# Normalising one batch's 4x4 matrices inside the other batch's attention

## The reference

```python
def step(carry, _):
    u, v = carry
    u = -jax.nn.logsumexp(Z + v[..., None, :], axis=-1)
    v = -jax.nn.logsumexp(Z + u[..., :, None], axis=-2)
    return ((u, v), None)
(u, v), _ = jax.lax.scan(step, (u0, v0), None, length=num_iters)
H_res = jnp.exp(Z + u[..., :, None] + v[..., None, :])
...
H_res = (1.0 - g) * I + g * H_res
x_pre = jnp.einsum('btnc,btn->btc', x_streams, H_pre)
y = x_pre @ W_branch
x_mixed = jnp.einsum('btij,btjc->btic', H_res, x_streams)
y_distributed = jnp.einsum('btc,btn->btnc', y, H_post)
return (x_mixed + y_distributed).reshape(B, T, nC)
```

## Time and profile before

| what | value |
|---|---|
| median of 3 runs | 2467.94 us (2463.57 to 2469.21) |
| the profiled execution, its own time | 2463.85 us |
| its span | 2461.6 us |
| PE busy | 2233.0 us (91%) |
| DVE busy | 1554.9 us (63%) |
| ACT busy | 1046.4 us (43%) |
| POOL busy | 1012.0 us (41%) |
| mean bandwidth | 67 GB/s, DMA engines 18.8% busy |
| chain that ended last | PE 32%, DVE 2%, issue 1%, ACT 1% of the span |

### The profile page before, as it was taken

How to read it: one execution, slowest core, us unless ns; L and a number is a source line. 1 busy time by engine, 2 the same in 40 slices (tenths; PEclk the granted TensorE clock), 3 DMA queues, 4 the chain that set the end, 5 groups by cost and what they waited for, 6 DMA issues and landing times. The chain is left out here.

```text
span 2461.6 us, 35450 instructions
## 1 busy us (share of the span) xinstructions
PE 2233.0 (91%) x11154; PEld 1814.2 (74%) x11154; DVE 1554.9 (63%) x3685; ACT 1046.4 (43%) x2182; POOL 1012.0 (41%) x1038
## 2 busy tenths in 40 slices
PE   5767449899999999999999796999999999999998
PEld 4633137688888888888887684788888888888886
DVE  4289875466666666666766455566565756566665
ACT  4322213354545444454545232444454545454543
POOL 2644351264545455363634100435262525343341
PEclk9878779899999999999999998999999999999999
DMA  9500035501010101101010434201101010101010
GB/s 341 189 9 1 0 140 209 207 26 66 9 65 9 65 26 48 56 17 56 26 48 1 166 131 185 86 27 43 47 21 51 26 56 13 60 9 60 18 38 31
DMA packets 74003, 164.83 MB, mean 67 GB/s; under 512 B 4704, under 2 KB 38880, under 8 KB 67296
## 3 DMA queue, kind: packets, MB, share of 16 engines
q1 hardware_dynamic: 73504, 162.69, 18.8%
q10 hardware_dynamic: 432, 1.32, 0.1%
HBM read 113.14 MB, written 72.61 MB: 75 GB/s over the span
## 5 line engine op out<-in xcount | busy, mean ns | idle before, releaser
L1521 DVE TENSOR_TENSOR pT<-psum,pT 128x512 fp32r<-128x512 f32 x576 | 387.0, 689 | 282.4 <-ACT pT L1562 281.6
L1474 POOL TENSOR_TENSOR probs_even<-probs_even,rinv 128x1024 f32<-128x1024 f32 (+2 forms) x192 | 241.0, 1255 | 677.5 <-DVE rinv L1512 677.5
L1562 ACT ACTIVATE pT<-psum 128x512 fp32r<-128x512 f32 x576 | 329.2, 596 | 299.1 <-PE psum L1615 299.0
L1507 DVE CUSTOM_DVE_ANT_0 psum<-psum,causal 128x256 f32<-128x256 f32 (+7 forms) x512 | 386.0, 767 | 38.1 <-PE psum L95 33.3
L1474 POOL TENSOR_TENSOR probs_odd<-probs_odd,rinv 128x896 f32<-128x896 f32 (+2 forms) x192 | 198.6, 1042 | 303.0 <-DVE rinv L1512 302.9
L1556 ACT ACTIVATE probs_even<-psum,nmax 128x1024 f32<-128x1024 f32 (+3 forms) x256 | 204.5, 799 | 250.1 <-DVE nmax L1507 246.2
L93 PE MATMUL psum<-keys,q 128*128 128x512 f32 (+3 forms) x768 | 265.6, 346 | 3.7 <-DVE q L1495 2.8
L95 PE MATMUL psum<-keys,q 128*128 128x512 f32 (+3 forms) x768 | 262.0, 341 | 0.0
L94 PE MATMUL psum<-keys,q 128*128 128x512 f32 (+3 forms) x768 | 261.9, 341 | 0.0
L93 PE MATMUL psum<-pT,vals 128*128 128x512 f32 x576 | 256.3, 445 | 3.9
L1556 ACT ACTIVATE probs_odd<-psum,nmax 128x896 f32<-128x896 f32 (+3 forms) x256 | 176.7, 691 | 148.1 <-DVE nmax L1507 145.9
(11 more groups left out here) (272 smaller groups left out, 4410.5 us busy)
## 6 DMA issues: line engine op xcount, KB each, us to landing
k_parts<-kv_out SPq DMA_DIRECT2D x32, 512.0 KB, 4.9
wq<-wq_copy SPq DMA_DIRECT2D x16, 1024.0 KB, 4.8
wo<-wo_copy SPq DMA_DIRECT2D x16, 1024.0 KB, 4.8
v_parts<-kv_out SPq DMA_DIRECT2D x32, 512.0 KB, 3.9
keys<-k_parts SPq DMA_DIRECT2D x32, 512.0 KB, 4.8
vals<-v_parts SPq DMA_DIRECT2D x64, 256.0 KB, 3.1
acc<-in_x SPq DMA_DIRECT2D x4, 1024.0 KB, 12.3
xn_later<-xn SPq DMA_DIRECT2D x1, 2048.0 KB, 14.5
```

Source lines behind the costliest of these rows:

```text
L1474: pool.tensor_tensor(p, p, rinv[:, u, h:h + 1].to_broadcast([P, (TB - u) * P]), ALU.mult).then_inc(p_ok, 1)
L1507: dve.tensor_tensor_reduce(out=row, in0=row, in1=causal[:, S - n:S], scale=-1.0, scalar=-2 * MASKED, op0=ALU.add, op1=ALU.min, accum_out=n ...
L1521: dve.tensor_tensor(pT[:, n % PT_SLOTS, 1, :], bank[T_BANK + n % 2], f32(pT[:, n % PT_SLOTS, 0, :]), ALU.subtract).then_inc(t_lo, 1)
L1562: act.activation(pT[:, n % PT_SLOTS, 0, :], bank[T_BANK + n % 2], ACT.Copy).then_inc(t_hi, 1)
```

## The change

Only batch 0's eight tiles are normalised in `layer0_mix`; a part of the loop is now 4 tiles (128x64 elements). `PER_UNIT` becomes 27 and the additions come at 14 to 17. The additions that fall after half round 98 (tile 11's and the last unit's) are done between the steps of the mixing. Of the mixing of batch 0, DVE keeps six tiles, and POOL gets tiles 6 and 7 (`BY_POOL`), 20 instructions of 128x512. The matrices of batch 1 are centred here but their 98 half rounds run in batch 0's attention: 20 in each of the iterations 0, 1, 3 and 4 and 18 in iteration 2 (`LATER_HALVES`). POOL does the product after a normalisation of heads 0 to 2, from block 1 on (block 2 on in iteration 2), and DVE the sum and the reciprocal (`factor`) behind its own reciprocal of the next such head. After 40 half rounds DVE folds the factors into `z1` (`recentre`), with ACT's Ln and Exp, and in iteration 5 it finishes the matrices (`finish`). The mixing of batch 1's eight tiles, on POOL as before, is gathered in iterations 5 (three tiles), 6 (three) and 7 (two); a pair now comes after each head of 0 to 2 from block 1 on, with two pauses of no work after each tile. DVE's and ACT's iterations of batch 0 are written out.

```diff
+LATER_CHUNKS, LATER_HALVES = (20, 29), (20, 20, 18, 20, 20)
...
+        Z, K = sb("sk_z", [P, NT, NS, NS]), sb("sk_k", [P, TB, NS, NS])
...
-        PER_UNIT = 23
+        PER_UNIT = 27
+        BY_POOL = 2
...
+            pool.wait_ge(mix_ok, 1)
+            for t in range(TB - BY_POOL, TB):
+                x = x1[:, t, :].rearrange("p (i c) -> p i c", i=NS)
+                pool.wait_ge(x1_ok, t + 1)
+                for j in range(NS + 1):
+                    n = 2 * ((NS + 1) * (t - (TB - BY_POOL)) + j)
+                    stream = xn[:, t, j * D:(j + 1) * D] if j < NS else y[:, t, :]
+                    weight = T[:, t, :, j] if j < NS else rw[:, t, 1, :]
+                    if j == NS:
+                        pool.wait_ge(y_ok, t // 4 + 1)
+                    if n:
+                        pool.wait_ge(pooled, n)
+                    pool.tensor_tensor(product[:], stream.unsqueeze(1).to_broadcast([P, NS, D]),
+                                       weight.unsqueeze(2).to_broadcast([P, NS, D]), ALU.mult).then_inc(pooled, 1)
+                    pool.wait_ge(pooled, n + 1)
+                    pool.tensor_tensor(x, x, product[:], ALU.add).then_inc(pooled, 1)
...
+            after(dve.tensor_tensor(Z[:, 0:TB], Z[:, 0:TB], wide_cols(v[:, 0:TB]), ALU.subtract))
+            after(dve.tensor_tensor(m.z1[:], Z[:, TB:NT], wide_cols(v[:, TB:NT]), ALU.subtract))
...
-                behind = PER_UNIT * (unit + 1) + 16 if unit + 1 < UNITS else 2 * sum(CHUNKS) - UQ
-                between.setdefault(behind + k, []).append((add_heads, t))
+                between.setdefault(PER_UNIT * (unit + 1) + 14 + k, []).append((add_heads, t))
...
+            ours = T[:, 0:TB]
+            after(dve.tensor_tensor(ours, K[:], wide_rows(row[:, 0:TB]), ALU.mult))
+            after(dve.tensor_tensor(ours, ours, wide_cols(col[:, 0:TB]), ALU.mult))
...
-            for k in range(0, TB, 2):
+            mixes, at = 0, 2 * sum(CHUNKS)
+            ready = {t: (x1_ok, t + 1) for t in range(NT)}
+            for k in range(0, TB - BY_POOL, 2):
                 for j in range(NS + 1):
                     for t in (k, k + 1):
...
+                        ready[t] = mixed, mixes
+                        for step, unit_tile in between.pop(at, ()):
+                            step(unit_tile)
+                        at += 1
...
-                        if t == 8:
-                            logs()
...
+                if unit == 1:
+                    logs()
...
+            tiles_of = {5: (0, 1, 2), 6: (3, 4, 5), 7: (6, 7)}
...
+                return iter(range(sum(LATER_HALVES[:it]), sum(LATER_HALVES[:it + 1])))
...
-            def loads(it, g):
...
                 load(wq[:, 1], m.wq_s[g]).then_inc(wq_in, 16)
+                for t in mixed_now[:2]:
+                    later_loads(t + 1)
...
+                for t in mixed_now[2:]:
+                    later_loads(t + 1)
...
+                loads(it, it + 1, tiles_of.get(it, ()) if mixes_later else ())
+            if mixes_later:
+                later_loads(TB - 1)
...
-                    yield
                     pool.wait_ge(mixed, n + 1)
                     pool.tensor_tensor(x, x, product[:], ALU.add).then_inc(mixed, 1)
                     yield
...
-                        if h == REP - 2 and 2 <= u:
-                            next(beside, None)
+                        if mixes_later and u >= first_pause(it):
                             next(beside, None)
...
+            def scaling(it):
+
+                for half in halves_of(it):
+                    if half == 2 * LATER_CHUNKS[0]:
+                        pool.wait_ge(k_ok, 1)
+                    pool.wait_ge(factor_ok, factors(half))
+                    pool.tensor_tensor(T1, m.k1[:], over_rows(m.row1) if half % 2 else over_cols(m.col1), ALU.mult).then_inc(scaled, 1)
+                    yield
+
+            def mixings(it):
+                if it == mixing_from:
+                    pool.wait_ge(share_ok, 1)
+                for t in tiles_of[it]:
+                    yield from mixing(t)
+                    yield
+                    yield
...
+                    body(it, it == ITERS - 1, scaling(it) if it < mixing_from else mixings(it))
...
+            def factor(half):
+
+                dve.wait_ge(scaled, half + 1)
+                by = T1 if half % 2 == 0 else T1.rearrange("p t i j -> p t j i")
+                dve.tensor_reduce(m.sm1[:], by, AX.X, ALU.add).then_inc(summed, 1)
+                dve.wait_ge(summed, half + 1)
+                dve.reciprocal((m.col1 if half % 2 else m.row1)[:], m.sm1[:]).then_inc(factor_ok, 1)
...
+            def recentre():
...
+                dve.tensor_tensor(m.z1[:], m.z1[:], over_rows(m.lrow1), ALU.add).then_inc(z_ok, 1)
...
+                dve.tensor_tensor(m.z1[:], m.z1[:], over_cols(m.lcol1), ALU.add).then_inc(z_ok, 1)
+                dve.memset(m.col1[:], 1.0).then_inc(factor_ok, 1)
...
+            def finish():
...
+                dve.wait_ge(factor_ok, factors(halves))
+                dve.tensor_tensor(T1, m.k1[:], over_rows(m.row1), ALU.mult).then_inc(share, 1)
...
+                dve.tensor_tensor(T1, T1, over_cols(m.col1), ALU.mult).then_inc(share, 1)
...
+                dve.tensor_scalar(mix, mix, m.gate[:, 2:3], None, ALU.mult).then_inc(share, 1)
...
+                dve.tensor_scalar(mix[:, :, 0:NZ:NS + 1], mix[:, :, 0:NZ:NS + 1], m.gate[:, 3:4], None, ALU.add).then_inc(share_ok, 1)
...
+                        if mixes_later and (u, h) == (1, 0):
+                            if it == turning:
+                                recentre()
+                            if it == mixing_from:
+                                finish()
                         if h == REP - 1:
 
                             p = probs[u % 2][:, h, 0:(TB - u) * P]
                             dve.wait_ge(p_inv, it * SC + (REP * u + h + 1))
                             dve.tensor_scalar(p, p, rinv[:, u, h:h + 1], None, ALU.mult).then_inc(p_last, 1)
+                        if mixes_later and (h < REP - 1 or u == TB - 1) and (u, h) > (first_pause(it), 0):
+                            half = next(beside, None)
+                            if half is not None:
+                                factor(half)
...
+            if mixes_later:
+                dve.memset(m.col1[:], 1.0).then_inc(factor_ok, 1)
+                for it in range(ITERS):
+                    body(it, it == ITERS - 1, halves_of(it))
...
+                        if mixes_later and it == turning and (u, h) == (1, REP - 1):
+                            act.wait_ge(z_ok, 2)
+                            act.activation(m.k1[:], m.z1[:], ACT.Exp).then_inc(k_ok, 1)
...
+                for it in range(ITERS):
+                    if it == turning:
+                        act.wait_ge(factor_ok, factors(2 * LATER_CHUNKS[0] - 1) + 1)
+                        act.activation(m.lrow1[:], m.row1[:], ACT.Ln).then_inc(logs_ok, 1)
+                        act.activation(m.lcol1[:], m.col1[:], ACT.Ln).then_inc(logs_ok, 1)
+                    body(it, it == ITERS - 1)
```

87 lines of the change are left out of this document (53 added, 34 removed).

## The result

The changed kernel takes 2486.14 us (median of 4 runs, 2485.34 to 2487.2) where the kernel before takes 2468.57 (4 runs, 2463.57 to 2471.56): ratio 1.0073, 95% interval 1.0056 to 1.0091. It is slower, as forecast, and 9 us under the 2495 of the forecast. Spans of the profiled executions: 2461.6 before, 2483.4 after, 21.8 more.

A forecast was written before the change was run, and what follows sets the result against it. DVE was taken to bound the first stage's mixing, PE the attention. First stage 15 us less (-28 + 13), attention 43 more: +28 on the median 2467.94 gives 2496, stated as 2495 us, range 2468 to 2514.

The forecast's parts named there:

- The half rounds: First stage's loop: smaller parts shorten each of 97 half rounds by 0.29 us, 28 us less (19 to 34).
- Zero in sum: First stage's additions: three earlier calls wait 4 us in all, the last unit's 4.39 us wait goes; no net change.
- The mixing: Batch 0's mixing: DVE's 30 us and POOL's 23.4 exclude each other, so 53.4 us, 13.4 more than before.
- Iterations 0 to 4: Batch 0's attention: half rounds in DVE's list delay PE's inputs; 20 us over iterations 0, 1, 3, 4, plus 5 in iteration 2.
- The last normalisation in block 7: Attention, block 7: three factors and another POOL wait ahead of it delay PE; 1.2 us counted per iteration.
- Iteration 2: Batch 0's attention: `recentre` beside POOL's normalisation costs 1.5 us in block 1, block 7 costs 1.8; 5 us taken.
- The cause named for blocks 2 to 4: Attention: a factor ahead of the last low copy makes PE wait; 0.6 us in block 2, 0.5 in 3 and 4.
- Lockstep: Rival, attention: factors and products wait for each other in every block, 10 us more an iteration, 2520 us; chance 0.1.
- Iterations 5 to 7: Batch 0's attention: POOL's mixing pairs delay the last wo part, 5 us stall each; with later blocks and `finish`, 18 us.

The follow-up runs named there:

- pool_mixes_four: Against the changed kernel, GpSimd mixes four of batch 0's tiles instead of two, DVE four, and the last unit's additions come slightly earlier; 2498.46 us.
- psum_operand: Against the changed kernel, DVE's 120 mixing operations read the operand they add to from PSUM, not SBUF, leaving out a sum over streams; 2466.15 us.
- no_half_rounds: Against the changed kernel, batch 1's 98 half rounds and the refolding are left out of the attention on POOL, DVE and ACT; 2464.90 us.
- pairs_from_block2: Against the changed kernel, POOL's mixing pairs in iterations 5 to 7 begin in block 2, not 1, with one pause per tile; 2482.29 us, ratio 1.0069.

## Why the prediction was right, and where it was off

The large terms came from the mechanisms that were named, and the experiments show them. Some single amounts came out right by errors that cancel, as is said at each.

*The half rounds.* Right in its parts; the term was short by 0.04 us a half round, 97 x 0.33 = 32 in place of 28. The three durations fell by 0.31, the handovers by the rest.

*"Zero in sum" for the additions* was wrong. They waited 2.15, 2.15 and 2.02 us, not 1.3, so 6.3 against the 4.39 that went: 2 us more. And I counted five additions neither as leaving the loop (-3.3) nor as arriving in the mixing (+3.3).

*The mixing.* The phase took about the 53.4 us predicted, but by luck: three errors cancel. Before, it lasted 42.1 us, not 40: I read 40.00 busy in a window that I had cut at 328.3, while the last operations ran to 330.4. The row itself counts 153 instructions, not 160. So the operations take 0.263 and 120 of them 31.6. The additions add 3.3. And the exclusion costs 18.6, not 23.4, because about one DVE operation comes through per POOL instruction. That the two exclude each other was right, and its price a quarter too high; the difference against before was +11.4, not +13.4. By the Trainium skill ("SBUF — State Buffer", section "Who interferes with whom") whoever issues first keeps the shared pair for its instruction. The trace agrees for both POOL operations, at 1.26 us per DVE operation against 0.26, and so does the kernel with one input in PSUM, which that rule leaves out of the conflict. POOL loses too, as the rule allows, but little: its three multiplications of 1.17 and 1.18 us in place of 1.05 began just behind a DVE operation, seven of 20 are as slow in pool_mixes_four, and none in psum_operand. An operation of 0.34 us holds POOL up for 0.12, an instruction of 1.05 to 1.26 holds DVE up for 0.9.

*Iterations 0 to 4.* 25 us predicted, 24.7 measured, and no_half_rounds gives all of it to the half rounds. By blocks of iteration 1, from when PE starts the same matmul in both kernels: 1.5 in block 1 (1.9 predicted), 0.6, 0.5, 0.6 and 0.4 in blocks 2 to 5 (0.6, 0.5, 0.5 and 0.3), 0.6 in block 6 (nothing) and 0.7 in block 7 (1.2). The path in blocks 6 and 7 was another than I had: factors ahead of a maximum and an addition make the addition late, and a query projection waits for it. The last normalisation in block 7, which I had blamed, delayed nothing that stayed. So the right sum of blocks 6 and 7 is luck. Iteration 2 lost 4.6 (5 predicted), of it 0.6 in block 1, where I had put 1.5 for `recentre`. The cause named for blocks 2 to 4, a factor ahead of the last low copy, was right and incomplete: the experiment that took it away met the same loss by way of the third maximum and ACT. Lockstep did not happen.

*Iterations 5 to 7.* 18 us predicted, 18.6 measured (7.7, 6.9, 4.0), or 20.1 if the last is taken to the end of the attention alone (5.5). The wait was 4.4 to 4.7, near the 5 predicted. What I had not counted is the clock behind it, 1.4 to 1.6 each time. In the last iteration two more things came, neither counted. PE has three waits there that no engine ends ("issue" in its timeline), 5.9 us together before and 3.7 now, which gave 2.1 back. And the last projection ran for 1.5 us longer at a lower clock. With `finish` ahead of them, the waits for low copies in block 1 of iteration 5 came to 1.3, some 1.0 more than in the kernel before; 1.2 had been put down for it.

*From the profile to the median.* I added the sum to the median and assumed that the profiled execution would again lie 4 us below it. It lay 0.8 below. Of the 9 us between forecast and result some 6 are terms of the sum (the spans differ by 21.8, not 28) and the rest is this.

## To carry to other kernels

Work put into an engine that is idle a third of the time is free or costly by its place alone: list the gaps of the in-order queue in the trace, put one piece into each, and follow a delay through every engine whose list it enters, since here a late maximum came back as a late copy on another engine. Before work is handed to GpSimd beside DVE, look at where both read: with two SBUF operands on DVE, each GpSimd instruction of 1.2 us took 0.93 us from DVE, and none with one operand in PSUM. When a phase is timed by a window, see that the window holds all of it and nothing else.

## What was not expected of the hardware

A stall of PE can cost more than itself. In iteration 5 of the changed kernel PE waited 4.38 us, until 1083.39; then the granted clock fell:

```profile
1054.60:1083.40 28.80, 23.02 (x125) 18.81 (x123) 21.03 (x42) 15.56 (x29) 23.81 (x19) 1.00 0.10 36
1083.40:1088.40 5.00, 5.00 (x17) 4.04 (x18) 0.00 (x0) 0.00 (x0) 3.58 (x3) 0.66 0.00 0
```

From 1084.0 to 1087.6 a pass of 512 columns took up to 0.63 us in place of 0.39 (mean clock 0.66 in the window, so mostly the lower level of 1.2 GHz). From the start of the projection to PE's next transposition it took 4.44 us (1083.39 to 1087.83), in the kernel before 2.84 (1074.68 to 1077.52): 1.6 us lost again. It is not the same each time: in the eight kernels that have these three waits the stretch took 4.2 to 5.3 us. After the waits of 2.6 us in pairs_from_block2 the same is seen, a mean clock of 0.61 from 1108.6 to 1113.0, and its iteration 5 was 9.7 us longer than 113.2 with 6.7 us of waits. Behind the waits of 0.3 to 1.1 us in the iterations with half rounds the clock stayed at 1.00. The length of the wait does not decide alone: ahead of the last projection of the attention PE waits 2.10 us for DVE's addition in both kernels, and the clock fell only in the changed one. Before, then after:

```profile
1376.30:1379.40 3.10, 3.01 (x12) 2.17 (x12) 0.00 (x0) 0.00 (x0) 0.00 (x0) 1.00 0.00 0
...
1397.80:1402.40 4.60, 4.56 (x12) 3.31 (x12) 0.00 (x0) 0.00 (x0) 0.00 (x0) 0.63 0.00 0
```

What made the difference there, no run shows.
